# A token list of 48 two-tile slots and 9 one-tile slots in place of 56 two-tile slots

## The reference, cut to what matters

```python
logits = xt @ Wr + br                                  # xt: 6250 x 256, 8 experts
top_p, top_idx = top_k(softmax(logits), 2)
weights = top_p / top_p.sum(axis=-1, keepdims=True)
xn = (xt - mu) * rsqrt(var + eps)
xe = xn[None] * ln_g[:, None, :] + ln_b[:, None, :]
h = gelu(einsum('end,edh->enh', xe, W1) + b1)          # 256 -> 1024
y = einsum('enh,ehd->end', h, W2) + b2                 # 1024 -> 256
out = (weights * y of the two chosen experts).sum()    # added to the token's row
```

## Time and profile before

| | us |
|---|---|
| median of 3 runs | 1983.86 (1983.77 to 1987.33) |
| the profiled execution's own time | 1983.19 |
| its span in the trace | 1981.5 |
| PE busy in the span | 1858.9 (94%) |
| DVE, ACT, POOL busy | 1345.8, 747.0, 1145.8 |
| first product of the experts, line 2497, x2688 | 305.1 |
| second product of the experts, line 2516, x2688 | 302.4 |
| list stage, DVE from its first operation to `slot_token` | 1313.2 to 1345.0 |
| expert stage, first POOL copy to the end of the span | 1346.0 to 1981.5 |

### The profile page before, as it was taken

The page is one execution under the profiler, slowest core; times in us unless marked ns, Lnnn a source line. Parts: engine busy times, 40 slices in busy tenths (PEclk is TensorE's granted clock), DMA queues, the critical chain, the costliest instruction groups (busy, mean ns, idle before and its releaser), DMA issues. The chain is left out here.

```text
span 1981.5 us, 40591 instructions
## 1 busy us (share of the span) xinstructions
PE 1858.9 (94%) x13425; PEld 1223.1 (62%) x13426; DVE 1345.8 (68%) x3351; ACT 747.0 (38%) x1711; POOL 1145.8 (58%) x1208
## 2 busy tenths in 40 slices
PE   6689999999999989999999999937999999999997
PEld 5545555555555534545444444416998989999996
DVE  7877777777777624676666676685767666676664
ACT  6654444444454420111111112134444444444442
POOL 5327777666777716676666666204656555656553
PEclk9799999999999999999999999967999999999998
DMA  8465555555555557787778888742333323323322
GB/s 284 139 215 181 184 178 185 204 192 179 181 180 208 188 198 256 255 271 257 253 258 270 313 274 308 239 193 48 50 49 48 48 46 51 51 46 51 48 46 25
DMA packets 121512, 329.38 MB, mean 166 GB/s; under 512 B 20448, under 2 KB 73312, under 8 KB 114464
## 3 DMA queue, kind: packets, MB, share of 16 engines
q0 software_dynamic: 59072, 142.05, 27.1%
q1 hardware_dynamic: 48192, 172.73, 24.4%
q10 hardware_dynamic: 14112, 12.85, 1.9%
HBM read 214.10 MB, written 113.45 MB: 165 GB/s over the span
## 5 line engine op out<-in xcount | busy, mean ns | idle before, releaser
L977 PE MATMUL mp_o<-rows,m_counts 128*128 128x512 f16 x1960 | 487.5, 380 | 9.5 <-ACT m_counts L1103 9.5
L620 POOL DMA_INDIRECT m_x_even<-rows_d,take_src x311 | 371.9, 1196 | 166.6 <-PE mp_x L990 117.6
L1973 PE MATMUL rp_o<-rows,adj_ring 128*128 128x512 f16 x1960 | 456.0, 380 | 8.8 <-issue 8.8
L1882 POOL DMA_INDIRECT r_took<-rows_d,take_src x311 | 324.0, 1042 | 176.7 <-PE rp_g L1989 117.1
L1103 ACT ACTIVATE m_counts<-mp 128x490 f16<-128x490 f32 (+4 forms) x544 | 291.6, 559 | 322.2 <-PE mp L1006 308.8
L1973 PEld LDWEIGHTS rp_o<-rows,adj_ring 128*128 128x128 f16 x1960 | 192.0, 98 | 225.8 <-issue 11.3
L2497 PE MATMUL fp_h<-f_xt,w 128*128 128x256 f16 x2688 | 305.1, 274 | 0.3 <-DVE f_xt L2593 0.3
L854 DVE TENSOR_TENSOR m_oh_lane<-lane_b,m_edge_lane 128x1920 f16<-128x1920 bf16 x171 | 198.4, 1160 | 154.5 <-PE mp L1006 152.5
L2516 PE MATMUL fp_y<-w,f_hh 128*128 x2688 | 302.4, 273 | 0.0
L977 PEld LDWEIGHTS mp_o<-rows,m_counts 128*128 128x128 f16 x1960 | 181.4, 97 | 185.7 <-issue 12.1
L2497 PEld LDWEIGHTS fp_h<-f_xt,w 128*128 x2688 | 264.3, 98 | 31.6 <-issue 0.7
(11 more groups left out here) (260 smaller groups left out, 1797.1 us busy)
## 6 DMA issues: line engine op xcount, KB each, us to landing
adj<-m_counts SPq DMA_DIRECT2D x40, 1568.0 KB, 5.8
adj_ring<-adj SPq DMA_DIRECT2D x40, 800.0 KB, 5.1
adj_ring<-adj SPq DMA_DIRECT2D x40, 768.0 KB, 5.1
r_raw<-in_L_ffn_W_dram POOLq DMA_DIRECT2D x16, 1024.0 KB, 9.1
w_parts<-r_parts POOLq DMA_DIRECT2D x8, 1024.0 KB, 6.6
w<-w_parts SPq DMA_DIRECT2D x4, 2048.0 KB, 10.4
rows<-in_x_turned_dram SPq DMA_DIRECT2D x7, 896.0 KB, 5.9
rows_d<-rows SPq DMA_DIRECT2D x7, 896.0 KB, 5.5
```

The lines of the kernel that those rows point to most:

```text
L620: pool.indirect_dma_start(out=took[:, r, :], out_offset=None, in_=k.rows_d[0], in_offset=bass.IndirectOffsetOnAxis(ap=k.take_src[:, i:i + ...
L977: mm = nc.tensor.matmul(ps_o[q], counts[:, q, s, :], k.rows[0][:, s, :], start=i == 0, stop=i == BLOCKS - 1)
L1882: pool.indirect_dma_start(out=took[:, r, :], out_offset=None, in_=k.rows_d[1], in_offset=bass.IndirectOffsetOnAxis(ap=k.take_src[:, i:i + ...
L1973: mm = nc.tensor.matmul(ps_o[b % 2], adj[:, m % ADJ_RING, at:at + P], rows[:, s, :], start=s == 0, stop=s == BLOCKS - 1)
```

## The change

The worst case is now counted in tiles: (12544 + 8 x 127) / 128, rounded down, is 105 tiles. 48 slots stay pairs (96 tiles), and 9 slots of one tile each follow (`SINGLES`), 57 slots in all (`UNITS`). An expert takes whole pairs for its entries and one single tile for a remainder of at most 128. The list stage works out both kinds of slot and moves each entry past the end of its expert's pairs to its single tile (`past`, `shift`). In `build_experts` the turns of pairs are 12 instead of 14, and behind the last one stand nine written-out slots with functions of their own on each engine; the last turn of pairs now also gathers and transposes for the first singles. The diff, cut:

```diff
-PAIRS = (2 * PAD_NODES + EXPERTS * (PAIR - 1)) // PAIR
-TOKEN_TILES = 2 * PAIRS
-SLOTS = TOKEN_TILES * P
+ALL_TILES = (2 * PAD_NODES + EXPERTS * (P - 1)) // P
+PAIRS = 48
+SINGLES = ALL_TILES - 2 * PAIRS
+UNITS = PAIRS + SINGLES
+TOKEN_TILES = ALL_TILES + ALL_TILES % 2
...
+            nc.vector.tensor_scalar(unit_at[:, 0:PAIRS], k.lane_f[0:1, 0:PAIRS], float(PAIR), None, ALU.mult)
+            nc.vector.tensor_scalar(unit_at[:, PAIRS:], k.lane_f[0:1, 2 * PAIRS:ALL_TILES], float(P), None, ALU.mult)
+            nc.vector.memset(apart[:], 1.0)
...
-            chain(nc.vector.tensor_scalar(cnt[:], cum[:, :, BLOCKS - 1], float(PAIR - 1), None, ALU.add))
+            chain(nc.vector.tensor_scalar(cnt[:], cum[:, :, BLOCKS - 1], float(P - 1), None, ALU.add))
             chain(nc.vector.tensor_copy(cnt_i[:], cnt[:]))
-            chain(nc.vector.tensor_single_scalar(cnt_i[:], cnt_i[:], 8, ALU.arith_shift_right))
-            chain(nc.vector.tensor_copy(tiles[:], cnt_i[:]))
-            chain(nc.vector.tensor_tensor_scan(ends[:], going[:, 0, 1:1 + EXPERTS], tiles[:], 0.0, ALU.mult, ALU.add))
+            nc.vector.tensor_single_scalar(tiles_i[:, 0], cnt_i[:], 8, ALU.arith_shift_right)
+            chain(nc.vector.tensor_single_scalar(tiles_i[:, 1], cnt_i[:], 7, ALU.arith_shift_right))
+            chain(nc.vector.tensor_single_scalar(tiles_i[:, 1], tiles_i[:, 1], 1, ALU.bitwise_and))
+            chain(nc.vector.tensor_copy(tiles[:], tiles_i[:]))
+            chain(nc.vector.tensor_tensor_scan(ends[:].rearrange("p k e -> p (k e)"), apart[:].rearrange("p k e -> p (k e)"),
+                                               tiles[:].rearrange("p k e -> p (k e)"), 0.0, ALU.mult, ALU.add))
+            nc.vector.tensor_scalar(single[:], ends[:, 0, EXPERTS - 1:], 2.0, float(2 * PAIRS), ALU.mult, ALU.max)
+            nc.vector.tensor_scalar(ends_at[:], ends[:, 0], float(PAIR), None, ALU.mult)
+            nc.vector.tensor_tensor(cum[:], cum[:], tot[:], ALU.subtract)
             chain(nc.vector.tensor_tensor(begin[:], ends[:], tiles[:], ALU.subtract))
-            chain(nc.vector.tensor_scalar(begin[:], begin[:], float(PAIR), None, ALU.mult))
-            chain(nc.vector.tensor_tensor(cum[:], cum[:], tot[:], ALU.subtract))
-            chain(nc.vector.tensor_tensor(cum[:], cum[:], bc(begin[:, :, None], [P, EXPERTS, BLOCKS]), ALU.add))
+            nc.vector.tensor_scalar(shift[:], begin[:, 1], single[:, 0:1], float(P), ALU.add, ALU.mult)
+            chain(nc.vector.tensor_scalar(begin_at[:], begin[:, 0], float(PAIR), None, ALU.mult))
+            nc.vector.tensor_tensor(shift[:], shift[:], ends_at[:], ALU.subtract)
+            chain(nc.vector.tensor_tensor(cum[:], cum[:], bc(begin_at[:, :, None], [P, EXPERTS, BLOCKS]), ALU.add))
             chain(nc.vector.tensor_tensor(ranks[:], ps_in[:].rearrange("p (b e) -> p b e", e=EXPERTS),
                                          cum[:].rearrange("p e b -> p b e"), ALU.add))
+            per_expert = [P, BLOCKS, EXPERTS]
+            chain(nc.vector.tensor_tensor(past[:], ranks[:], bc(ends_at[:, None, :], per_expert), ALU.is_ge))
+            chain(nc.vector.tensor_tensor(past[:], past[:], bc(shift[:, None, :], per_expert), ALU.mult))
+            chain(nc.vector.tensor_tensor(ranks[:], ranks[:], past[:], ALU.add))
...
-            chain(nc.vector.tensor_tensor(le[:], bc(ends[0:1, None, 0:EXPERTS - 1], [1, PAIRS, EXPERTS - 1]),
-                                         bc(k.lane_f[0:1, 0:PAIRS, None], [1, PAIRS, EXPERTS - 1]), ALU.is_le))
+            chain(nc.vector.tensor_scalar(single_end[:], ends[0:1, 1], single[0:1, 0:1], float(P), ALU.add, ALU.mult))
+            units = [1, UNITS, EXPERTS - 1]
+            for n, at in enumerate((ends_at[0:1], single_end[:])):
+                below = nc.vector.tensor_tensor(le[:, n], bc(at[:, None, 0:EXPERTS - 1], units), bc(unit_at[:, :, None], units), ALU.is_le)
+            nc.vector.tensor_scalar(in_pair[:], unit_at[:], ends_at[0:1, EXPERTS - 1:], None, ALU.is_lt)
+            nc.vector.memset(k.pair_expert[:], 0)
+            chain(below)
             chain(nc.vector.tensor_reduce(te[:], le[:], AX.X, ALU.add))
-            nc.vector.memset(k.pair_expert[:, 0:1], 0)
-            nc.vector.memset(k.pair_expert[:, 1 + PAIRS:], 0)
-            nc.vector.tensor_copy(k.pair_expert[:, 1:1 + PAIRS], te[:])
+            chain(nc.vector.tensor_tensor(te[:, 0], te[:, 0], in_pair[:], ALU.mult))
+            nc.vector.tensor_tensor(k.pair_expert[:, 1:1 + UNITS], te[:, 0], te[:, 1], ALU.add)
...
+            def destinations(a, e):
+
+                pool.wait_ge(added, 16 * a)
+                hold_waits(k, nc.gpsimd, 1 + 3 * M)
+                nc.gpsimd.tensor_copy(to[:, 0:e - a], k.slot_token[:, a:e]).then_inc(to_staged, 1)
+                pool.wait_ge(to_staged, PAIR_TURNS + 1 + (a - 2 * PAIRS) // (2 * M))
+                hold_waits(k, nc.gpsimd, 2 + 3 * M)
+
+            destinations(2 * PAIRS, 2 * PAIRS + 2 * M)
+            end = ALL_TILES - 1
+            pool.wait_ge(got[0], 16 * (PAIR_TURNS + 1))
+            pool.wait_ge(x_t, end - 2 * M + 1)
+            pool.wait_ge(gated, end - 2 * M + 1)
+            hold_waits(k, nc.gpsimd, 0)
+            nc.gpsimd.tensor_copy(stage[:, 0:1], k.slot_token[:, end:end + 1]).then_inc(staged, 1)
+            pool.wait_ge(staged, PAIR_TURNS + 2)
+            pool.indirect_dma_start(out=xg[:, 0, :], out_offset=None, in_=k.xn_rows,
+                                    in_offset=bass.IndirectOffsetOnAxis(ap=stage[:, 0:1], axis=0)).then_inc(got[0], 16)
+            for i in range(SINGLES):
+                if i == 2 * M:
+                    destinations(tile_of(i), tile_of(i) + 1)
+                addition(tile_of(i))
+            pool.wait_ge(added, 16 * ALL_TILES)
...
+            def transposes_single(i):
+
+                t = tile_of(i)
+                pe.wait_ge(*got_at(t))
+                pe.wait_ge(x_aff, t - 1)
+                for c in range(KF):
+                    mm = nc.tensor.transpose(ps_x[i % 2][:, c * P:(c + 1) * P], xg[:, t % (2 * M), c * P:(c + 1) * P], k.ident[:])
+                mm.then_inc(x_t, 1)
+
+            def first_single(i, ex):
+                t, u = tile_of(i), PAIRS + i
+                pe.wait_ge(x_hi, t + 1)
+                pe.wait_ge(x_lo, t + 1)
+                for b in range(HBANKS):
+                    pe.wait_ge(act_done, unit_banks(u - 1, b))
+                    for j in range(PER_BANK):
+                        h, n = b * PER_BANK + j, 0
+                        for wh, xh in SPLITS:
+                            for c in range(KF):
+                                w = k.w[:, bass.ds(ex, 1), 0, wh, c * HIDDEN + h * P:c * HIDDEN + (h + 1) * P][:, 0, :]
+                                mm = nc.tensor.matmul(ps_h[b][:, j * PAIR:j * PAIR + P], w, xt[:, u % 2, xh, c, 0:P],
+                                                      start=n == 0, stop=n == 5)
+                                n += 1
+                    mm.then_inc(up, 1)
+
+            def second_single(i, ex):
+                t, u = tile_of(i), PAIRS + i
+                pe.wait_ge(y_done, t - 1)
+                n = 0
+                for b in range(HBANKS):
+                    pe.wait_ge(h_hi, unit_banks(u, b))
+                    pe.wait_ge(h_lo, unit_banks(u, b))
+                    for h in range(b * PER_BANK, (b + 1) * PER_BANK):
+                        for wh, xh in SPLITS:
+                            w = k.w[:, bass.ds(ex, 1), 1, wh, h * D:(h + 1) * D][:, 0, :]
+                            mm = nc.tensor.matmul(ps_y[i % 2][:], hh[:, u % 2, xh, h, 0:P], w, start=n == 0, stop=n == 3 * HB - 1)
+                            n += 1
+                mm.then_inc(down, 1)
+
             every(nc.tensor, turn)
+            for i in range(SINGLES):
+                m = i % M
+                if m == 0:
+                    ex = experts(nc.tensor, regs, PAIR_TURNS + i // M)
+                if i < SINGLES - 1:
+                    transposes_single(i + 1)
+                first_single(i, ex[m + 1])
+                if i == 0:
+                    second_product(PAIR_TURNS - 1, M - 1, ex[0], True)
+                else:
+                    second_single(i - 1, ex[m])
+            second_single(SINGLES - 1, ex[(SINGLES - 1) % M + 1])
...
+            def halves_single(i):
+                u = PAIRS + i
+                dve.wait_ge(down, tiles_through(u - 2))
+                for b in range(HBANKS):
+                    part = slice(b * PER_BANK, (b + 1) * PER_BANK)
+                    dve.wait_ge(act_done, unit_banks(u, b))
+                    nc.vector.tensor_copy(hh[:, u % 2, 0, part, 0:P], h32[:, part, 0:P]).then_inc(h_hi, 1)
+                    dve.wait_ge(h_hi, unit_banks(u, b))
+                    nc.vector.tensor_tensor(hh[:, u % 2, 1, part, 0:P], h32[:, part, 0:P], hh[:, u % 2, 0, part, 0:P],
+                                            ALU.subtract).then_inc(h_lo, 1)
+
...
```

(72 more changed lines are left out.)

67 lines of the change are left out of this document (59 added, 8 removed).

## The result

The changed kernel takes 1958.7 us (median of 4 runs, 1955.68 to 1962.34), the kernel before 1983.8 in the same comparison. The ratio is 0.9874, 95% interval 0.9852 to 0.9895, so 21 to 29 us less: faster by 25. A second comparison gave 1959.3 and a ratio of 0.9884 (0.9867 to 0.9900). The forecast of 1956.5 is 2.2 to 2.8 us too low; both medians lie in the range that was given for that case (1952 to 1960).

The account below looks back on a forecast made before the run. PE was taken to bound the expert stage, and its sequencer the singles; PE -26.8, list +2.4 and tail -2.9 sum to -27.3 us, giving 1956.5 us. Forecast case 1952 to 1960 (0.60), whole range 1943 to 1966.

Parts of the forecast that it names:

- PE's sequencer is the bound in the singles: Singles: register operations at some 124 ns each set PE's pace, 6.7 us a single in place of 5.6 by columns.
- rival 1: Singles: PE runs at its columns, register operations hidden, 5.6 us for every single; 1946 us in all; chance 0.17.
- The lead: PE's sequencer starts the singles 1.6 us ahead, full behind slot 47's second product; single 0 takes 8.8 us, single 1 5.8.
- Singles 2 to 7: Six singles without lead, at the sequencer's pace: 6 x 6.7 = 40.2 us.
- PE's side: Expert stage from the end of common work: 65.8 us in place of 92.6, so -26.8 us.
- The list stage: DVE's dependent chain gets longer by wide and small operations: +2.4 us, bounds +1.5 and +3.5.
- The tail: After PE's last matmul, POOL has caught up but the last additions still follow each other: -2.9 us, bounds -5.4 and 0.
- Rival 2: Singles: sequencer slower in a full stream, 0.5 to 1.0 us a single, +4 to +9 in all, 1960 to 1965; chance 0.12.
- Rival 3: Singles: PE's clock falls to 1.2 GHz, 10.7 us a single, all nine give 1992; chance 0.06 with other new waits.
- Rival 4: Nine singles' straight code comes late; 2.5 us lost in each would leave 1979; chance 0.05 with the like.
- The two figures for 128 columns: Trainium skill: 55.6 to 56 ns for matmuls alone, about 81 ns with weight loads; by the second, first product 3.9 us.

Follow-up runs that it names:

- the repeated run: The changed kernel unaltered, run once more beside the runs that leave something out: 1959.3 us, ratio 0.9884 against the kernel before.
- the experiment: Changed kernel with one of four weight blocks of the singles' first product at a fixed address, 24 register operations in place of 32: 1955.1 us, ratio 0.9857.

## Why the prediction was right, point by point

The sum forecast was -27.3; from the list on it was -23.1, and -23.6 in the repeated run. That the medians came within 2.2 and 2.8 us is in part luck. -23.1 on the first comparison's 1983.8 would be 1960.7, just outside 1952 to 1960; 1958.7 was measured, and the layers ahead of the list scatter by up to 10 us. The second comparison's 1982.8 with -23.6 gives 1959.2, as measured.

- **PE's sequencer is the bound in the singles: right.** With the operations gone a single takes 5.52 us, about rival 1's figure (5.6); with them 7.0. The 124 ns read off eight rows at the half clock hold at the full clock: 118 ns by the experiment, 125 by the rows of the changed kernel. A first product came to 4.15 us and the transposes ahead of it to 0.22, 4.4 together; the 4.25 forecast was for both.
- **The lead: right.** Singles 0 and 1 took 8.8 and 5.8 us, as forecast (the terms given for single 0 add up to 8.6; the 8.8 measured has 0.22 of transposes in it), and when a pair stands between, the lead is there again.
- **Singles 2 to 7: mis-sized, 6.7 forecast, 7.0 measured.** 48 operations at 124 ns are 5.95 us; the rest of a single (waits, matmuls without an operation) I put at 0.7, and it is 1.05 with 48 operations as with 40 (6.05 - 4.96 = 1.09). Most of the 0.3 is the second product: I took the 2.4 us of its sequencer, and it lasted 2.63, its columns' time; about 0.1 is the first product with its transposes. Over six singles 1.8 us. The last single was 0.3 longer and the two reads of the experts 0.2 shorter in sum. PE's side: 67.6 us where 65.8 was forecast, -25.0 against -26.8. The -25.7 of the trace has 0.9 of something else in it, the first slot of the stage, which begins at the half clock (a granted clock of 0.52 from 1350 to 1360 in before, 1.00 from 1360 on; 0.62 from 1350 to 1357 in the changed kernel). This is its first product, in the chain of before and in that of the changed kernel, where 5.24 is the full clock's time:

```profile
1354.43 7.91 PE fp_h L2497 x48
```

```profile
1351.93 7.03 PE fp_h L2572 x48
```

In the repeated run of the changed kernel the same piece took 6.42 us. It is chance, as far as these runs show, and no gain of the change.

- **The list stage: +1.9 against +2.4**, within its bounds. The wide operations came to the 0.6 each with link; some of the small ones lay beside others.
- **The tail: -2.7 against -2.9**, as worked out: tile 103's addition at 1938.55 lands 3.82 later, the copy of the last destination (0.13) and its holds follow, and the last addition is issued at 1943.55.
- **Missing from the sum: POOL's drain, +3.4.** The span of before ends 7.1 us behind the issue of the last addition, and I took those 7.1 us as a constant that both kernels share. 2.27 of them were a drain, and in the changed kernel it takes 5.66. This is the larger part of the miss.
- **Rival 1** (PE at its columns) had the right price for PE without operations, and the wrong condition. **Rival 2** (a slower sequencer in a full stream) is out: the operations keep their 124 ns, and a single took 0.3 us more than forecast, most of it the second product's columns, where the rival had 0.5 to 1.0 for matmuls without an operation. **Rival 3** (the clock falls): 1.00 throughout the singles. **Rival 4** (straight code comes late): the straight code of nine singles ran without a gap once the operations were gone.
- **The two figures for 128 columns.** A weight load and a matmul at 128 columns took 56 ns as a pair, in nine products of 48. So the 56 ns that the Trainium skill ("TensorE: Matmul & The Clock Gate", Back-to-back issue gap) gives for the isolated gap agrees with the runs even with a load ahead of every matmul, and the same section's 81 ns for such a stream doesn't: the 4.15 us of a first product, 86 ns a matmul, looked like it and had another cause.

## What to carry to other kernels

In these runs each new address that depends on a register cost PE's sequencer some 124 ns, the same at 128 columns as at 256; so halving the columns took the engine's time down only to the sequencer's pace. Count these operations, take their pace from a stretch where the queue is empty, and set them against the columns; where they are more, place the short work between long work, or let several instructions use one address. And when a kernel's end is compared, count what lies behind the last DMA too: a drain there can differ by more than a part of the change brings.

## What the hardware showed that was not expected

- POOL's drain behind indirect DMAs is exact for a given program and differs between programs: 5659 ns in all seven traces with 210 of them in the expert stage (both orders of the slots among them), 2515 with 217 in both orders, 2270 and 3087 with 224.
- A busy PE row can hide a late stream: 48.18 of 50 us busy at 86 ns a matmul, where 56 was possible. The weight loads' busy time (77% against 95% in the same singles with fixed addresses) and the start-to-start times showed it.
- The two layers ahead of the list took up to 10 us more or less from one execution to another (1307.5 to 1318.1) with code that no kernel here changed; most of the spread between executions lies there.
